# A four-layer fp32 transformer kernel: LoRA adapter matrices and layer 2's column vectors loaded as rows and turned on VectorE, and layer 0's output weights requested earlier on the load queue

## The reference, cut to what matters

```python
xn = _layernorm(x)                       # before each layer
x = x + attn(xn) + ffn(xn)               # four times, each with its own kind
# layer 0: 32 heads of 16, rotary, causal; out = heads @ wo.T
# layer 0's feed-forward: 4-bit weights, 512 -> 1376 -> 512
# layer 1: b_qkv, b_o;   layer 3: wq_b, wk_b, wv_b, wo_b (bias vectors)
# layer 2: q = rms_norm(xn @ Wq + bq, gq), k likewise with bk, gk; v with bv (each 4096 long)
def _lora_linear(x, w, a, b):            # layer 2's feed-forward, rank 16
    return x @ w.T + ((x @ a.T) @ b.T) * 2.0
h1 = _lora_linear(x, w1, lora_A1, lora_B1)   # w1, w3 [1376, 512]; B1, B3 [1376, 16]
h3 = _lora_linear(x, w3, lora_A3, lora_B3)   # A1, A3 [16, 512]
y  = _lora_linear(silu(h1) * h3, w2, lora_A2, lora_B2)   # A2 [16, 1376]; B2 [512, 16]
```

## Time and profile before

| what | value |
|---|---|
| median of 3 runs | 2640.35 us (2630.17 to 2642.89) |
| the profiled execution | 2640.22 us |
| its span, first to last instruction | 2638.4 us |
| TensorE busy, mean granted clock | 2465.9 us (93%), 0.972 |
| VectorE / ScalarE / GpSimd busy | 1667.7 / 1032.4 / 942.2 us |
| DMA packets, of them under 512 B | 477241, 351476 |

### The profile page before, as it was taken

One profiled execution on the slowest core, in us unless ns is written; L12 is line 12 of the kernel. 1 busy time (PEld: TensorE's weight loads), 2 busy tenths in 40 slices (PEclk: granted clock), 3 DMA queues, 4 the chain that ended last, 5 costly groups with the idle time before them and its releaser, 6 DMA issues. The chain is left out here.

```text
span 2638.4 us, 40741 instructions
## 1 busy us (share of the span) xinstructions
PE 2465.9 (93%) x14448; PEld 1968.3 (75%) x14448; DVE 1667.7 (63%) x2382; ACT 1032.4 (39%) x2030; POOL 942.2 (36%) x581
## 2 busy tenths in 40 slices
PE   6999999689969989999999979999999999999899
PEld 4777766568855668888888868888888887888566
DVE  5886556465466776544444447787878886543576
ACT  3332144343144543223333344444455454323453
POOL 3342200137330135114444445544555544430000
PEclk8999999899989999999999989999999999999899
DMA  2232369722315213224444332222222222322430
GB/s 84 60 110 73 69 82 75 43 41 47 60 38 88 53 32 51 44 68 147 146 146 144 119 101 90 87 80 63 83 78 85 72 45 38 53 47 35 96 65 33
DMA packets 477241, 195.94 MB, mean 74 GB/s; under 512 B 351476, under 2 KB 430716, under 8 KB 477114
## 3 DMA queue, kind: packets, MB, share of 16 engines
q1 hardware_dynamic: 424584, 193.52, 30.9%
q10 hardware_dynamic: 52530, 0.70, 3.0%
HBM read 129.43 MB, written 44.04 MB: 66 GB/s over the span
## 5 line engine op out<-in xcount | busy, mean ns | idle before, releaser
L598 PE MATMUL banks<-xn_hi,w_hi 128*128 128x512 f32 x1264 | 496.5, 393 | 10.3 <-ACT sgf L1141 8.5
L598 PE MATMUL banks<-xn_hi,w_lo 128*128 128x512 f32 x1264 | 493.5, 390 | 0.0
L598 PE MATMUL banks<-xn_lo,w_hi 128*128 128x512 f32 x1264 | 493.1, 390 | 0.0
L598 PEld LDWEIGHTS banks<-xn_hi,w_hi 128*128 128x128 f32 x1264 | 238.2, 188 | 61.6 <-DVE w_lo L586 9.3
L598 PEld LDWEIGHTS banks<-xn_hi,w_lo 128*128 128x128 f32 x1264 | 237.8, 188 | 49.9
L598 PEld LDWEIGHTS banks<-xn_lo,w_hi 128*128 128x128 f32 x1264 | 238.2, 188 | 48.4
L3066 POOL TENSOR_TENSOR qk_raw<-qk_raw,rms 128x1024 f32<-128x1024 f32 x64 | 158.9, 2484 | 272.0 <-DMA qk_raw<-qk_scratch 260.4
L586 DVE TENSOR_TENSOR w_lo<-tw,w_hi 128x512 fp32r<-128x512 f32 (+2 forms) x136 | 117.7, 872 | 201.3 <-ACT w_hi L578 201.2
L1253 POOL TENSOR_TENSOR h_lo<-sgf,h_hi 128x512 fp32r<-128x512 f32 (+1 forms) x94 | 128.2, 1368 | 287.7 <-ACT h_hi L1144 287.7
L2657 POOL TENSOR_TENSOR ssq<-ssq,sq 128x512 f32<-128x512 f32 x128 | 165.3, 1292 | 183.0 <-ACT sq L2628 183.0
L2645 DVE TENSOR_SCALAR raw<-banks,cols 128x512 f32<-128x512 f32 x128 | 103.6, 810 | 180.3 <-ACT sq L2628 180.3
(11 more groups left out here) (296 smaller groups left out, 5866.9 us busy)
## 6 DMA issues: line engine op xcount, KB each, us to landing
qk_scratch<-raw SPq DMA_DIRECT2D x64, 512.0 KB, 3.0
qk_raw<-qk_scratch SPq DMA_DIRECT2D x64, 512.0 KB, 3.8
nat<-in_L_ffn_w SPq DMA_DIRECT2D x48, 256.0 KB
head_scratch<-stage SPq DMA_DIRECT2D x16, 512.0 KB, 3.2
st_qs<-st_hi SPq DMA_DIRECT2D x64, 128.0 KB, 2.6
nat<-in_L_attn_Wq SPq DMA_DIRECT2D x32, 256.0 KB
nat<-in_L_attn_Wk SPq DMA_DIRECT2D x32, 256.0 KB
nat<-in_L_attn_Wv SPq DMA_DIRECT2D x32, 256.0 KB
```

The costliest lines, as they stand in the source:

```text
L598: mm = nc.tensor.matmul(to[half][:, :], w[0:n, j, k * P:(k + 1) * P], r, start=first and k == 0 and x == 0, stop=last and k == len(rows) - ...
```

## The change

- `sp_units` takes a range. SP now issues units 0 to 2, then the four loads of `wo0`, then units 3 to 7, then B1 and B3, then the columns.
- A B matrix is loaded in rows: partition i of 32 gets 43 (B2: 16) consecutive rows of 16 floats, one run of 2752 B (B2: 1024 B), three times for three groups of 32 partitions, into the bytes of the adapter's own bf16 target. VectorE turns 32x32 blocks of it (each row of 16 read twice) into all 96 rows of `lora_f`, 16 blocks an instruction; for B1, B3, B2 the spread copies are gone. The A matrices are loaded and spread as before.
- VectorE turns B1 in iteration 10 and B3 in iteration 11 of `att0`, and after B3 all of `cols2` in one instruction (`dve_columns`); B2 in group 3 of `att1`, where SP issues its load before the head loads.
- The column loads are 19 DMAs instead of 38; the five of layer 2 go as rows of 32 floats to `col_nat`. ScalarE waits for the turned columns.
- `pool_adapters_clear` moves from after `att0` to before it, and waits for the stores of the heads.
- ScalarE issues no adapter load any more.

```diff
+        _, col_nat = arena(("at_pad", [P, 27392]), ("col_nat", [P, 5, H2]))
+        def dve_columns(dve):
+            dve.wait_ge(cols_in.sem, cols_in.count)
+            nc.vector.transpose(cols2[:, :, :], col_nat[:, :, :]).then_inc(cols_turned.sem, 1)
 # sp_columns
-            for kv in range(KV1):
-                rows = slice(kv * HD, (kv + 1) * HD)
-                get(bias1[rows, 0:QC], b[kv * QC * HD:(kv + 1) * QC * HD].rearrange("(c d) -> d c", d=HD))
-            for n in range(2):
-                get(bias1[:, QC + n:QC + n + 1], b[D + n * P:D + (n + 1) * P].rearrange("(d o) -> d o", o=1))
+            for c in range(QC):
+                get(bias1[:, c:c + 1], b[0:D].rearrange("(v c d) -> c v d", c=QC, d=HD)[c])
+            get(bias1[:, QC:QC + 2], b[D:D + 2 * P].rearrange("(n p) -> p n", p=P))
-                for r in range(DUP):
-                    get(bias3[r * HD:(r + 1) * HD, QC + n:QC + n + 1],
-                        t[f"L3_attn_{name}_b"].rearrange("(d o) -> d o", o=1))
+                get(bias3[:, QC + n:QC + n + 1], t[f"L3_attn_{name}_b"].rearrange("(o d) -> o d", o=1).broadcast_to([DUP, HD]))
-                get(cols2[:, n, :], t[f"L2_attn_{name}"].rearrange("(h d) -> d h", d=P))
+                get(col_nat[:, n, :], t[f"L2_attn_{name}"].rearrange("(h a i) -> a h i", a=QUADS, i=QUAD))
 # dve_att, layer 0, after norm(i - 1)
+                if i in turns:
+                    dve_adapter(dve, turns[i])
+                    if i == max(turns):
+                        dve_columns(dve)
 # act_att
-                if i in loads:
-                    adapter_load(act, loads[i])
+        def dve_adapter(dve, s):
+            if s.free is not None:
+                dve.wait_ge(adapter_split.sem, s.free.done)
+            dve.wait_ge(adapter_in[s.buf].sem, s.loaded)
+            n, width = s.to.shape[1] // QUAD, s.to.shape[1]
+            src = adapter_rows(s).rearrange("p (k r) -> p k r", r=RANK)
+            dst = lora_f[s.buf][0:LORA_ROWS, 0:width].rearrange("p (i k) -> p k i", i=QUAD)
+            for k0 in range(0, n, 16):
+                k = slice(k0, min(k0 + 16, n))
+                ins = nc.vector.transpose(dst[:, k, :], src[:, k, :].unsqueeze(2).broadcast_to([LORA_ROWS, k.stop - k0, 2, RANK]))
+            ins.then_inc(adapter_turned.sem, 1)
 # adapter_load
+            if s.rows:
+                for x in range(0, LORA_ROWS, QUAD):
+                    eng.dma_start(adapter_rows(s)[x:x + QUAD, :], s.src[0][2].rearrange("(i k) r -> i (k r)", i=QUAD))\
+                      .then_inc(adapter_in[s.buf].sem, 16)
+                return
 # SP's program
-            sp_units(sp, att0)
-            sp_columns(sp)
+            sp_units(sp, att0, range(UNIT_SLOTS))
             sp_proj(sp, wo0, True)
             sp_proj(sp, wo0)
-            sp_adapter_spread(sp, adapters[0])
-            sp_adapter_spread(sp, adapters[1])
+            sp_units(sp, att0, range(UNIT_SLOTS, UNITS))
+            sp.wait_ge(cleared.sem, 4)
+            adapter_load(sp, adapters[0])
+            adapter_load(sp, adapters[1])
+            sp_columns(sp)
...
+            adapter_load(sp, adapters[3])
             sp_att(sp, att1)
-            sp_adapter_spread(sp, adapters[3])
 # ScalarE's and VectorE's programs
-            act_att(act, att0, wo0, {2: adapters[0], 8: adapters[1]})
+            act_att(act, att0, wo0)
-            act.wait_ge(cols_in.sem, cols_in.count)
+            act.wait_ge(cols_turned.sem, cols_turned.count)
-            act_att(act, att1, wo1, {1: adapters[3]})
+            act_att(act, att1, wo1)
-            dve_att(dve, att0, wo0)
+            dve_att(dve, att0, wo0, {10: adapters[0], 11: adapters[1]})
-            dve_att(dve, att1, wo1)
+            dve_att(dve, att1, wo1, {3: adapters[3]})
```

More of the change, by code:

```diff
@@ L307, in build @@
         adapter_in = [sig(f"adapter_in{x}", "sp") for x in range(2)]
+        cols_turned = sig("cols_turned", "dve")
+        adapter_turned = sig("adapter_turned", "dve")
         adapter_spread = [sig(f"adapter_spread{x}", "sp") for x in range(2)]
@@ L2128, in sp_k_split, with sp_units @@
             sp.wait_ge(k_split.sem, f.k0 + 2 * (tile + 1))
[L2130 to L2134, removed]
+        def sp_units(sp, s, units):
+            if 0 in units:
+                for j in range(SLOTS):
+                    sp.wait_ge(stage_out[j].sem, in0.st0[j] + 16 * len(PIECES) // SLOTS)
+            for u in units:
                 half, c = divmod(u, QC)
@@ L2415, in pe_att, with dve_att @@
                     shift(i + 1, part)
-        def dve_att(dve, s, wo):
+        def dve_att(dve, s, wo, turns):
             def top(i, part):
@@ L2467, in dve_att @@
                     joint_tops(g + 2, 9, JSTEPS)
+                    if g in turns:
+                        dve_adapter(dve, turns[g])
                     if g == n_g - 2:
@@ L2499, in att_out, with act_att @@
             return x[:, chunk, seq * SEQ:(seq + 1) * SEQ]
-        def act_att(act, s, wo, loads):
+        def act_att(act, s, wo):
             def shift_queries(i):
@@ L2551, in act_att @@
                                 act_hi(act, wo, m, m, ALL)
-                    if g in loads:
-                        adapter_load(act, loads[g])
                     if g == n_g - 2:
@@ L3086, in plan_adapter @@
             s.buf, s.free, s.src, s.to, s.side = buf, free, src, to, side
-            s.loaded = adapter_in[buf].reserve(16 * len(src)) + 16 * len(src)
-            s.spread = adapter_spread[buf].reserve(16 * 5) + 16 * 5
+            s.rows = src[0][2].shape[0] != RANK
+            n = LORA_ROWS // QUAD if s.rows else len(src)
+            s.loaded = adapter_in[buf].reserve(16 * n) + 16 * n
+            s.spread = None if s.rows else adapter_spread[buf].reserve(16 * 5) + 16 * 5
+            s.turned = adapter_turned.reserve(1) + 1 if s.rows else None
             s.ops = 7 + side
@@ L3092, in plan_adapter, with adapter_rows @@
             return s
-        def adapter_load(eng, s):
+        def adapter_rows(s):
+            return s.to[0:LORA_ROWS, :].bitcast(F32)
+        def dve_adapter(dve, s):
[9 more added lines that the diff above has]
+            ins.then_inc(adapter_turned.sem, 1)
+        def adapter_load(eng, s):
+            if s.rows:
[3 more added lines that the diff above has]
+                return
             if s.free is not None:
@@ L3114, in pool_adapter @@
             for n in range(s.ops) if ops is None else ops:
-                if n == 0:
+                if n == 0 and s.rows:
+                    pool.wait_ge(adapter_turned.sem, s.turned)
+                elif n == 0:
                     pool.wait_ge(adapter_spread[s.buf].sem, s.spread)
@@ L3204, in build @@
         wo1 = plan_proj(wo(t["L1_attn_w_o"], bias1, True), "blocks", KT, rhs_out(heads1), "dve", tw=tw_wo1)
-        adapters = [plan_adapter(0, None, [(0, F0, t["L2_ffn_lora_B1"].rearrange("o r -> r o"))], bst[:, 0, 0:F0], 0),
-                    plan_adapter(1, None, [(0, F0, t["L2_ffn_lora_B3"].rearrange("o r -> r o"))], bst[:, 1, 0:F0], 0)]
+        adapters = [plan_adapter(0, None, [(0, F0, t["L2_ffn_lora_B1"])], bst[:, 0, 0:F0], 0),
+                    plan_adapter(1, None, [(0, F0, t["L2_ffn_lora_B3"])], bst[:, 1, 0:F0], 0)]
         adapters += [plan_adapter(0, adapters[0], [(0, D, t["L2_ffn_lora_A1"]), (D, D, t["L2_ffn_lora_A3"])],
                                   ast[:, :, :].rearrange("p a b -> p (a b)"), 1),
-                     plan_adapter(1, adapters[1], [(0, D, t["L2_ffn_lora_B2"].rearrange("o r -> r o"))], b2st[:, :], 0)]
+                     plan_adapter(1, adapters[1], [(0, D, t["L2_ffn_lora_B2"])], b2st[:, :], 0)]
         adapters += [plan_adapter(0, adapters[2], [(0, F0, t["L2_ffn_lora_A2"])], a2st[:, :], 1)]
@@ L3379, in _ @@
             barrier(act, "prep3")
-            act_att(act, att3, wo3, {})
+            act_att(act, att3, wo3)
             act_wo(act, wo3)
@@ L3421, in _ @@
             barrier(dve, "prep3")
-            dve_att(dve, att3, wo3)
+            dve_att(dve, att3, wo3, {})
             dve_wo(dve, wo3)
@@ L3436, in _ @@
             barrier(pool, "v0")
+            for j in range(SLOTS):
+                pool.wait_ge(stage_out[j].sem, in0.st0[j] + 16 * len(PIECES) // SLOTS)
+            pool_adapters_clear(pool)
             pool_att(pool, att0)
-            pool_adapters_clear(pool)
             pool_close(pool, norms[1])
```

## The result

The kernel after takes **2595.31 us** in the median (2593.06 to 2600.87, four runs), beside 2636.58 us for the kernel before on the same chip (2630.17 to 2642.89, four runs). The profiled execution took 2593.06 us, its span is 2591.2 us.

What follows compares the result with a forecast made beforehand. TensorE, busy 93% of the span, was taken as the bound, with idle stretches in and after attention 0. 2640.2 - 26.9 (holes) - 9.5 (stops) + 0.5 (turns) = 2604.3, predicted as 2604 us, range 2597 to 2619.

Steps and rivals of the forecast that it cites:

- The sum: Whole kernel: 2640.2 less 26.9 (holes) less 9.5 (stops) plus 0.5 (VectorE's turns) gives 2604.3 us.
- The base: Whole kernel before: its profiled execution's 2640.2 us, from which the gains were taken.
- the first case: Whole kernel: the forecast holds, 2602.6 to 2612 us by its own bounds; chance 0.70.
- The two holes: TensorE between attention 0 and layer 1: idle times of 11.6 and 10.4 us and cold products go, gain 26.9 us.
- The yardstick: Layer 1's same stretch after attention, 29.3 us less 0.9 of adapter products, taken as layer 0's new length, 28.4 us.
- The low bound of the stretch: Attention 0's end to layer 1: may take 27.2 us without layer 1's waits for adapter sums.
- the first hole: TensorE ahead of layer 0's output projection: 11.2 us waiting for late output weights, queued on SP behind 43.3 us of column issues.
- The stops in attention 0: Two long iterations, 16.85 and 10.10 us against 8.73, fall to the usual period; gain 9.5 us, other end 0.
- code that arrives late: TensorE's 4.78 us stop in attention 0 read as late instructions during four-byte B loads; rival that stops stay: 2613.5 us, 0.14.
- VectorE's turns: Attention 0 and 1: B1 and B3 2.9 us each, 7.4 us in sum, of which 0.5 on the path.
- The rival of dear turns: Attention 0: turns at 3 us each in place of 1.09 make VectorE the bound, 2619 us; chance 0.05.
- The new waits: VectorE in iterations 10 and 11 of attention 0: 7 us left for B1, 8 us for columns to land; no wait.

Runs made afterwards that it cites:

- e1: The kernel before, unchanged, run again for a second trace: 2628.94 us, ratio 0.9996 to the other runs of before.
- e5: The kernel after, unchanged, run again for a second trace: 2595.06 us (one run).
- e7: The kernel after with the columns loaded as before, 38 DMAs of single words, and no turn of them on VectorE: 2600.91 us, ratio 0.9873.
- e3: The kernel after with the output weights' loads put back behind the adapters and columns: 2596.1 us, ratio 0.9871.
- e2: The kernel before with only layer 0's output weights' loads moved behind unit 2; adapters and columns stay single words: 2606.7 us, ratio 0.9909.
- e8: The kernel after with each of VectorE's adapter turns (B1, B3, B2) done three times: 2602.53 us, ratio 0.9886.
- e12: The kernel after with GpSimd's first low part held until VectorE has added the squares of the layernorm's second half: 2592.18 us, ratio 0.9853.
- e10: The kernel after plus B1's single-word load to unread rows, issued in iteration 4 of attention 0 (about 393 us): 2595.22 us, one run.
- e11: The kernel after plus B1's single-word load to unread rows, issued in iteration 0 of attention 0 (about 358 us): 2596.16 us, one run.
- e6: The kernel after plus both B word loads of the kernel before, in iterations 2 and 8, to free rows: 2613.25 us, ratio 0.9916.
- e9: The kernel after plus B1's word load in iteration 2, into its old rows 0 to 15, VectorE's turn waiting for it: 2603.41 us, one run.
- e4: The kernel after plus one single-word load of B1 by ScalarE in iteration 2, to rows that nothing reads: 2599.35 us, ratio 0.9888.

## Why the prediction was right in its mechanism and wrong in its time

**The gain came out, in part by luck.** The sum took 26.9 + 9.5 - 0.5 = 35.9 us from the kernel. The touched stages of the profiled pair give 10.24 + 29.05 - 4.34 and 0.3 of small change, 35.2 us; between e1 and e5 it is 37.9. Single terms were too small by 2.1, 0.7 and 0.5 us, and a loss of 4.3 us that the sum did not have cancelled them.

**The base was wrong, and that is the step that failed.** "Against the profiled execution's own 2640.2 us" took one execution for the kernel. In the profiled pair the spans lie 47.2 us apart, 35.2 of them where the sum looked, and 12.0 in stages that the change does not touch: 11.4 in attention 2, 2.1 ahead of attention 0, and 1.5 the other way. With the base at 2640.2 and every touched stage as measured, the sum would still say 2605. Of the 14 traces here, 12 have 619 to 626 us in attention 2; 631.3 (before) and 634.2 (e7) are the two others.

How much of the 8.7 us the base explains in the medians is less clear. The four runs of before beside the kernel after have a median of 2636.6 us, and 2636.6 - 35.9 is 2600.7, inside the range; the 5.4 us down to 2595.3 are within the interval of the measured gain (32 to 49 us) and have no shown cause. All 36 runs of before that stood beside the kernels here have a median of 2631.8 us (2617.0 to 2645.5), which gives 2595.9, but they are from four chips, with medians from 2628.4 to 2636.6. I noted that the three runs lay 12.7 us apart and that the median equalled the trace, and then let only "a few us more" for scatter below the first case. A base known to 10 us asks for a low end of 2592, not 2597. (The upper end of that first case is also 1 us too low: 2640.2 - 25.1 - 9.5 + 7.4 is 2613, not 2612.)

**The two holes** (forecast 26.9, 25.1 to 28.1; measured 29.1). Both are gone. The yardstick, layer 1's stretch, was 2.1 us long: it is 29.3 us less adapter products, while layer 0's came out at 26.3 at full clock. The granted clock of that yardstick was 0.94, which I did not read; in e3 the same stretch of layer 1 has 1.00 and takes 27.8 us, so about 1.5 of the 2.1 us go with the clock. The low bound of the stretch, 27.2, was too high by 0.9. The reason for the first hole needs both halves: the output weights stood behind 43 us of column issues, and taking away either is enough. e2 moves the weights and keeps the words, e3 keeps the place and takes the words away, and in neither does a first hole remain.

**The stops in attention 0** (forecast 9.5; measured 10.2, or 11.1 between e1 and e5). All eight traces in which the B matrices were not fetched as words (after, e3, e5, e7, e8, e12), or B1 at another time (e10, e11), run attention 0 without a stop of issue; all six in which B1's words were issued near 375 us have one. Section Instruction fetch mechanics of the Trainium skill's page Runtime: NRT & Kernel Launch calls the crossing of a block of code mostly hidden; of these traces that holds for every one without the words near 375, and not for the others, by 1.25 to 6.15 us.

The traces say more: the stop ends when a block of code has landed. Queue q8 brings packets of 16384 bytes, 83 in the span, one for about 256 of TensorE's products and weight loads (the median between two packets is 256.5 in the kernel before). The first stop stands after the same 1460 of these in before, e1, e2, e6 and e9, and all other stops of issue stand after 1715, 1972 or 2739, which is 1, 2 or 5 steps of 256 further on, to within one instruction. In us since attention 0's first scores, for the block that TensorE needs at 66.9 to 67.8:

| trace | block begins to move | has landed | TensorE goes on | stop there |
|---|---|---|---|---|
| after, e10 | 55.3 | 56.2 | | none |
| e4 | 58.8 | 61.8 | | none (1.25 at the next block, landed at 74.8) |
| e11 | 58.9 | 62.6 | | none |
| e6 | 65.0 | 66.3 | 67.8 | 0.90 |
| e9 | 65.6 | 67.0 | 68.5 | 1.59 |
| e2 | 66.9 | 68.2 | 69.9 | 2.97 |
| before | 68.7 | 70.6 | 72.3 | 4.78 |
| e1 | 70.3 | 72.3 | 74.0 | 6.15 |

TensorE goes on 1.5 to 1.7 us after the landing, each time. In e10 the block began to move at 394.0, ahead of the first word at 395.4. In the kernel before no packet of q8 starts between 392.5 us and the start of the stop at 406.4, while the queue of the words has a share of 94.2%; one starts inside the stop (DMA queues, 406.37 to 411.15 us):

```profile
q8 instruction: 1, 0.02, 2.5%
```

So my reading, code that arrives late, is shown. The forecast price was of one pairing of load and code.

**VectorE's turns** (forecast 2.9 us per adapter, 0.5 on the path; measured 2.74 to 2.76 us and none). The 96x512 form takes 1125 ns each, the 96x352 form 827, the columns 329 (by form, the kernel after):

```profile
L3117 DVE STREAM_TRANSPOSE lora_f<-bst 96x512 f32<-96x512 f32 x4 | 4.2, 1125 | 0.0
L3117 DVE STREAM_TRANSPOSE lora_f<-bst 96x352 f32<-96x352 f32 x2 | 1.7, 827 | 0.0
L685 DVE STREAM_TRANSPOSE cols<-col_nat 128x160 f32<-128x160 f32 x1 | 0.3, 329 | 0.0
```

The rival of dear turns falls by these rows; e8 shows that its reasoning on the cover was right, since at three times the work 9.7 of 11.1 us came out.

**The new waits** (forecast none; none seen). The adapters landed 7.2 us after their issue, in the median of six, where the forecast had 7 us left for B1; in the trace VectorE asks for B1 at 442.4, 10 us after the last of its issues. e6 shows what a slower landing costs: with B3's words beside them the same loads cost 11.4 us of TensorE.

**What I did not foresee** is the loss of 4.3 us (2.5 between e1 and e5) in layer 1 behind the stretch. At most 0.8 us of it is GpSimd's operation beside VectorE's additions, by e12's one trace. The rest goes with the clock of the first 22 us, though not with the change alone: it is 1.00 in the kernel before (stage 245.9 us), 0.92 in e1, the same kernel (247.8), and 0.85 in the kernel after (250.3). What sets it is not settled: the wait for the squares is 1.8 us in before and e1 alike, and with 1.8 us the stage took 249.4, 246.8 and 248.2 us in e7, e8 and e9.

**Attention 2** was put down to wandering. Before's trace falls behind e5's there in three steps of 3 to 4 us, near 1666, 1743 and 1826 us, where TensorE waits 2.13, 3.91 and 3.92 us for VectorE's low parts of the weights; e1's longest wait of that kind is 1.72, and e7, the other long one, has two of 3.85. The second of these waits in before, VectorE's two operations ahead of it, and the same two in e1:

```profile
1743.38 0.49 PE L2839 MATMUL banks<-w_hi,xn_hi 128*128 128x512 f32 x1 [3.91 <-DVE w_lo L3018]
```

```profile
1737.59 5.66 DVE L3018 TENSOR_TENSOR w_lo<-nat,w_hi 128x512 fp32r<-128x512 f32 x2 [0.26 <-ACT w_hi L2948]
```

```profile
1741.38 3.46 DVE L3018 TENSOR_TENSOR w_lo<-nat,w_hi 128x512 fp32r<-128x512 f32 x2 [0.26 <-ACT w_hi L2948]
```

In both GpSimd works beside them; two of the same form take 1.28 us right after (at 1743.97 in before). What decides how the two engines fall together in one execution was not tried.

**Open.** Why the block moves 3 to 5 us later in the kernel before and in e1 than in e6 and e9, with the same word load at the same time. The rows that the words go to are not the reason (e9 has 3.15 us in two stops of issue, e6 2.46 with other rows), and the order of the output weights is at most a part of it (e2: 66.9).

## What to carry to other kernels

A load in single words that nothing waits for may cost nothing itself (e10, e11); what it takes is from others: the issue time of its queue, the landing of what is beside it, and, when a block of code is due behind it, the code. Fetch in rows and turn on an engine that has the slack, but count the slack in turns: here it was one a chunk. And before a gain is taken from a base, ask how far two executions of the kernel before lie apart stage by stage; the largest part of the difference between the two traces that the sum had not named was there, in a stage that nobody touched.

## What the runs showed of the hardware

- In attention 0 TensorE stopped between two products of one run, with no semaphore to wait for, in each of six traces in which a load of 22016 single words was issued near 375 us, and in none of the others; the same load 17 us earlier or 18 us later left no stop. The five stops at the first of these places ended 1.5 to 1.7 us after a 16384-byte packet of the instruction queue had landed.
- A B matrix of 22016 words took 36 to 56 us to land as single words. In e6 VectorE waited 13.4 us for column loads that were issued beside it.
- A transpose on 96 partitions that reads each row twice and writes words 172 bytes apart took 1125 ns for 512 columns, a plain one on 128 partitions 1085.
- Two additions of VectorE's, 128x512 in fp32, took 2.36 us beside an operation of GpSimd's of 1.36 us, and 1.49 us in e12, where that operation came later.
